# Attention with a banded mask and a routed MLP on one core: the output projection behind the first half's shift, its eviction between the exponentials, and three smaller moves

## The reference

```
x = x + attention(layernorm(x)) @ W_out + b_out      # 16 heads of 8, causal band of 32 keys
...
logits = layernorm(x) @ w_router                     # 8 choices, the best one is taken
sel    = expert e of 7 for a token, or none (choice 7)
x = x + 2 * prob(best) * expert_sel(h)               # (h @ w_up) * silu(h @ w_gate) @ w_down, 512 hidden
      + (h @ ws_up * silu(h @ ws_gate)) @ ws_down    # the shared expert, for all tokens
```

## Time and profile before

| what | value |
|---|---|
| runs | 309.22, 310.01 (median), 312.88 us |
| the profiled execution | 310.81 us, of which the span from first to last instruction is 308.8 us |
| mean granted TensorE clock | 0.991 |
| busy in the span | TensorE 293.2 us, VectorE 224.7, GpSimd 174.4, ScalarE 148.2 |
| attention, first maximum of round 0 to that of round 15 | 15.95 to 125.90 us |

### The profile page before, as it was taken

One profiled execution on the slowest core, in us unless ns is written; L12 is line 12 of the kernel. 1 busy time (PEld: TensorE's weight loads), 2 busy tenths in 40 slices (PEclk: granted clock), 3 DMA queues, 4 the chain that ended last, 5 costly groups with the idle time before them and its releaser, 6 DMA issues. The chain is left out here.

```text
span 308.8 us, 11890 instructions
## 1 busy us (share of the span) xinstructions
PE 293.2 (95%) x4834; PEld 242.9 (79%) x4834; DVE 224.7 (73%) x442; ACT 148.2 (48%) x230; POOL 174.4 (56%) x269
## 2 busy tenths in 40 slices
PE   8999999999799998889999999999989999999994
PEld 8846576657476666567888888889989999999993
DVE  5699999889779898876798655476677867865442
ACT  3544444545435476567273233244454554555530
POOL 6799476933214872391017777636467656655344
PEclk9999999999979999999999999999999999999998
DMA  7971414132313232109951233234244444334321
GB/s 195 338 194 55 109 44 119 47 108 53 97 42 109 50 98 62 56 15 392 345 158 55 91 114 111 88 73 86 62 85 95 87 88 96 73 80 82 72 51 27
DMA packets 52503, 32.46 MB, mean 105 GB/s; under 512 B 25424, under 2 KB 46676, under 8 KB 52450
## 3 DMA queue, kind: packets, MB, share of 16 engines
q1 hardware_dynamic: 47968, 23.18, 30.2%
q0 software_dynamic: 2880, 6.43, 6.0%
q10 hardware_dynamic: 1602, 2.10, 2.2%
HBM read 13.72 MB, written 11.95 MB: 83 GB/s over the span
## 5 line engine op out<-in xcount | busy, mean ns | idle before, releaser
L693 POOL DMA_INDIRECT out<-y,xn_base x38 | 38.6, 1015 | 38.9 <-DVE y L1390 37.7
L790 ACT ACTIVATE Pr<-psS 128x1024 f32<-128x1024 f32 x32 | 32.8, 1026 | 30.3 <-PE psS L1499 30.3
L1375 DVE TENSOR_TENSOR Pr<-psS,PT 128x512 f32<-128x512 f32 x38 | 26.1, 686 | 23.9 <-PE psS L1762 12.2
L907 ACT ACTIVATE PT<-psS 128x512 f32<-128x512 f32 x38 | 22.7, 597 | 38.9 <-PE psS L1762 30.2
L978 DVE TENSOR_REDUCE row_max<-psS 128x16 fp32r<-128x1024 f32 x32 | 37.7, 1218 | 4.8 <-PE psS L1487 4.7
L1760 PE MATMUL psS<-xT_hi,taken_parts 128*128 128x256 f32 x128 | 38.3, 299 | 0.0
L874 ACT ACTIVATE PT<-psS 128x512 f32<-128x512 f32 x32 | 19.1, 597 | 38.9 <-PE psS L1633 28.8
L1040 DVE STREAM_TRANSPOSE PT<-Pr 128x1024 f32<-128x1024 f32 x32 | 37.4, 1206 | 0.1
L1762 PE MATMUL psS<-xT_hi,taken_parts 128*128 128x256 f32 x128 | 36.1, 282 | 0.0
L536 POOL TENSOR_TENSOR rows<-rows,proj 128x256 f32<-128x256 f32 x15 | 10.9, 726 | 44.7 <-ACT proj L796 44.1
L1761 PE MATMUL psS<-xT_lo,taken_parts 128*128 128x256 f32 x128 | 35.9, 281 | 0.0
(11 more groups left out here) (227 smaller groups left out, 669.8 us busy)
## 6 DMA issues: line engine op xcount, KB each, us to landing
sorted_rows<-pad_rows SPq DMA_DIRECT2D x9, 528.0 KB, 6.1
xn_base<-sorted_rows SPq DMA_DIRECT2D x38, 66.0 KB, 1.9
rows<-in_L_attn_x SPq DMA_DIRECT2D x8, 256.0 KB, 6.0
xs<-sorted_rows SPq DMA_DIRECT2D x64, 32.0 KB
VD_even<-V SPq DMA_DIRECT2D x28, 72.0 KB, 2.8
VD_odd<-V SPq DMA_DIRECT2D x28, 72.0 KB, 2.5
w_sb<-in_L_ffn_w_gate ACTq DMA_DIRECT2D x1, 1792.0 KB, 12.8
Kx<-K SPq DMA_DIRECT2D x28, 64.0 KB, 2.2
```

Source lines behind the costliest of these rows:

```text
L693: pool.indirect_dma_start(out=out_list, out_offset=bass.IndirectOffsetOnAxis(tok_u[:, r, :], 0), in_=y[:, r, :], in_offset=None, bounds_ch ...
L790: nc.scalar.activation(Pr[:, half, :], psS[:, half, :], ACT.Exp, scale=SCALE).then_inc(exp_done, 1)
L1375: nc.vector.tensor_tensor(hs[:, k % PLACES, :], psS[:, k % 2, 0:512], sg[:, k % 2, :], ALU.mult).then_inc(eh_done, 1)
```

## The change

Four things are changed. In rounds 2 to 14 the output projection on TensorE stands behind the first half's shift (and behind `turn_x`) and no longer at the head of the round, and its copy on ScalarE stands behind the first exponential (and behind `evict_xnT`). The second block of idle matmuls has 24 in place of 48. The four copies that make `pick_h` go from GpSimd to VectorE, behind the statistics of the second batch, with a semaphore of their own. SP loads the fifth pair's tokens before it waits for the last scatters, where the four base loads stood ahead of them.

```diff
@@ SyncE
             for n in range(4):
                 load_pair(n)
+            load_pair(4)
             sp.wait_ge(base_scattered, 16 * LATE * TPB)
             for i in range(RING):
                 load_base(i, i, wait=False)
-            load_pair(4)
@@ GpSimd
             make(pool.memset(edge_h[:, :, BLK:], 0.0))
-            for g in range(NG):
-                w = slice(g * BLK, (g + 1) * BLK)
-                make(pool.tensor_copy(pick_h[w, :, :], ident[w, w].unsqueeze(1).to_broadcast([BLK, NJ, BLK])))
             make(pool.tensor_scalar(minus_ident[:, :], ident[:, :], -1.0, None, ALU.mult))
@@ ScalarE, pair(p)
-                if 2 <= p < NP - 1:
-                    evict_proj(p - 2)
                 exponentials(p, 0)
                 if p in (0, 2):
                     evict_xnT(n)
+                if 2 <= p < NP - 1:
+                    evict_proj(p - 2)
                 exponentials(p, 1)
@@ VectorE, after the statistics of the second batch
+            dve.wait_ge(filled, after["ident"])
+            for g in range(NG):
+                w = slice(g * BLK, (g + 1) * BLK)
+                nc.vector.tensor_copy(
+                    pick_h[w, :, :], ident[w, w].unsqueeze(1).to_broadcast([BLK, NJ, BLK])
+                ).then_inc(picks_ready, 1)
             dve.wait_ge(bias_mm, 1)
@@ TensorE
-            keep_warm(psS[:, 0, 0:P], 3 * WARM // 8)
+            keep_warm(psS[:, 0, 0:P], 3 * WARM // 16)
...
             pe.wait_ge(filled, after["masks"])
+            pe.wait_ge(picks_ready, NG)
...
-                if 2 <= p < NP - 1:
-                    project(p - 2)
                 if n == B:
                     turn_rows(2 * h + 1)
                 if p > 0:
                     weigh_values(p - 1, 0)
                 shift_scores(p, 0)
                 if p in (0, 2):
                     turn_x(n)
+                if 2 <= p < NP - 1:
+                    project(p - 2)
                 if p > 0:
                     weigh_values(p - 1, 1)
```

More of the change, by code:

```diff
@@ L237, in windowed_attention_top1_moe_kernel @@
         norm1_ready, first_normed = sem("norm1_ready"), sem("first_normed")
+        picks_ready = sem("picks_ready")
         first_k_ready, first_v_ready = sem("first_k_ready"), sem("first_v_ready")
```

## The result

The changed kernel takes 321.02 us in the median (320.06 to 323.36) against 310.33 us before (309.22 to 312.88), four runs of each: a ratio of 1.0384, 95% interval 1.0344 to 1.0423, so 10.7 us slower. The profiled execution has a span of 319.4 us and a mean granted clock of 0.993.

A forecast was written before the change was run, and what follows sets the result against it. VectorE was taken to set the quiet attention round, 6.33 us of work in 6.52. From the profiled 310.8 us, +16.8 (rounds) - 1.1 (start) - 1.2 (fifth pair) = 325.3, or 324.5 us as median; 8-in-10 range 319 to 332.

The forecast's parts named there:

- The mechanism: Rounds 2 to 14: copy behind first exponential makes VectorE's moments wait some 2 us for GpSimd's residual, near 26 us in all.
- Length of a round: Attention rounds 2 to 14: 6.33 us of VectorE work plus 2.03 us of later moments, 8.36 us a round.
- Round 2: Extra in round 2: input statistics (1.5 us for rounds 2 and 3 together) and the copy also behind `evict_xnT`, 0.5 us.
- The stop followed by half clock, +1.5: TensorE's longest stop, 2.0 us from 83.1, then 2.7 us at half clock: 1.5 us added, between 0 and 2.3.
- The start, -1.1: Kernel start: 24 idle matmuls fewer and picks on VectorE gain 1.1 us, between 0.4 and 1.4.
- my lower bound: Start gain of only 0.4 us, if the values' spreading DMAs land when they do today.
- The fifth pair, -1.2: SP's fifth-pair loads ahead of the scatter wait: VectorE's wait there goes, gain 1.2 us, between 0 and 1.3.
- The clock: Rival: VectorE-bound rounds idle TensorE, its clock falls to half; +6.5 us, 331 us, or 337 if scores become late; chance 0.12.
- the 0.5 us priced: Clock rival's estimate: at half clock a TensorE shift of 0.70 us takes some 0.5 us more in each of 13 rounds.
- TensorE's order: Rival: residual in time, but the projection's 0.64 us between the two shifts sets the price; +5.9, 313.5 us; chance 0.06.
- the covered wait: Rival: wait covered, rounds unchanged, only start and fifth pair change; 307.7 us; chance 0.04.
- TensorE's 0.64 us: Rounds 2 to 14: TensorE's 0.64 us is hidden by VectorE's wait; without that cover up to 0.6 us a round.

The follow-up runs named there:

- 12 tiny matmuls: Kernel before with start and fifth-pair edits, plus 12 tiny (32 x 32 by 32 columns) matmuls behind the 24 idle ones: 325.95 us, ratio 0.9890, on another chip.

## Why the prediction was right, and where it was off

The forecast was 324.5 us, 319 to 332; measured 321.0.

- *The mechanism*: right, to the wait. About 26 us of waiting for the residual was forecast, 26.2 us is in the trace; undoing the copy's place or moving the moments takes it away.
- *Length of a round*: forecast 8.36 us, measured 8.02 to 8.03. This is the largest mis-sized term, 13 x 0.34 = 4.4 us. Its error is one of reading. I chained reported durations: the exponential's 1.03 us to the copy (M+3.08), and VectorE's 6.33 us of work. On the chip each next instruction starts before the reported end of the one ahead: the copy 0.92 us behind the exponential's start, at M+2.90; the next maximum 2.25 us behind the start of two transposes of 2.33 us (78.07 to 80.32). The Trainium skill (Perfetto Trace Analysis, DVE / Act Engine Instruction) says that a reported end includes the acknowledgement of the write; the overlap of 0.08 to 0.11 us agrees.
- *Round 2*: 9.6 us by the terms of the forecast, 9.28 measured; the difference is the length of a round again, the extra statistics and the extra copy were sized right.
- *The stop followed by half clock, +1.5*: it did not happen in round 9 (8.02 us). Of the stops inside rounds 2 to 14 one of 0.64 us still shows, in a round of 8.08 us; the new slack covers the others. The two behind the start of round 15 are not covered, 0.89 and 1.60 us.
- *The start, -1.1*: the first maximum came 1.49 us sooner, round 2 0.95. As a part of the whole kernel's time it is worth nothing (ratio 1.0005). This step failed, though the total hides it: I carried a gain at the start to the end without asking what else the 24 removed instructions move. That is not all of it, since keeping the count didn't bring the gain back either. Part of the 1.49 us was never a gain: in the six profiles of kernels with the start as before, the first maximum lies anywhere from 14.98 to 16.16 us (mean 15.55) and round 2 begins at 30.24 in the mean; in the four with the changed start these are 14.63 and 29.81. By these means the edit is worth 0.9 us at the first maximum and 0.4 us at round 2. Where the rest goes stays open.

```profile
8.68 0.63 PE L1433 MATMUL psA<-ident,xn_base 128*128 128x128 f32 x4 [0.77 <-ACT xn_base L739]
...
9.57 1.45 DVE L1015 CAST pick_h<-ident 32x128 bf16<-32x128 f32 x4
...
14.46 1.23 DVE L976 TENSOR_REDUCE row_max<-psS 128x16 fp32r<-128x1024 f32 x1
...
23.12 0.76 PE L1523 MATMUL psO<-VD_even,PT 128*32 128x36 f32 x64 [1.16 <-DMA VD_even<-V]
```

  The rows are the changed kernel's first transpose of x, the four picks on VectorE (1.45 us for the four, as against 1.33 on GpSimd), the first maximum, and the first values, which now wait 1.16 us for their spreading DMAs, 0.46 before. That is the mechanism of my lower bound, and it takes part of the gain back.
- *The fifth pair, -1.2*: measured alone 1.7 us, 0.8 to 2.7. In the changed kernel the wait at the fifth pair is gone, and a later one of 1.09 us comes up at a later pair, within the bounds given:

```profile
236.69 0.43 DVE L1281 STREAM_TRANSPOSE xT<-xs 128x256 f32<-128x256 f32 x1
...
245.10 0.45 DVE L1281 STREAM_TRANSPOSE xT<-xs 128x256 f32<-128x256 f32 x1 [1.09 <-DMA xs<-sorted_rows]
```

- *The clock*: the rival did not decide, but it happened once. Where TensorE waited 1.26 and then 1.10 us in round 4, the granted clock fell to 0.50, the 1.2 GHz level, and rose again behind 52 us:

```profile
48.00:50.00 2.00, 1.12 (x3) 0.94 (x4) 1.96 (x2) 0.00 (x0) 0.00 (x0) 0.65 0.48 111
50.00:52.00 2.00, 2.00 (x69) 1.70 (x67) 0.00 (x0) 1.29 (x2) 0.49 (x1) 0.50 0.57 160
52.00:54.00 2.00, 2.00 (x13) 1.06 (x6) 1.67 (x7) 1.26 (x2) 2.00 (x6) 1.00 0.03 7
```

  A shift took 1.22 us there for 0.70, the 0.5 us priced, and round 4 took 8.59 us, 0.57 more than the rounds behind it. It was not the idle time of a usual round: round 4 alone had both gaps above 1 us. In rounds 5 to 14 they were at most 1.27 and 0.40 us, in round 3 0.90 and 1.10 us, and the clock stayed at 1.00.
- *TensorE's order and the covered wait*: both fell. With the copy moved alone the time is the same; with the projection moved alone the loss is that of the later copy. What the forecast said of TensorE's 0.64 us, hidden by the wait and up to 0.6 us a round without it, is borne out by the two kernels with late moments: 0.4 us in a quiet round.

In short, the rounds were priced 5.2 us too high (16.8 for 11.6), 4.4 of it for the length of a round and the rest for a stop that did not come, less the slow clock that came in round 4. On the other side, 1.2 us of gain was forecast behind the rounds and none is there in the profiled pair (182.9 us both): the stops of 0.89 and 1.60 us stand against the fifth pair's gain, which is argued from the rows and not isolated. So the total is nearer than its largest term by luck: one error took back part of the other. The forecast's own range, 321 to 328, holds the result at its edge.

## What to carry to other kernels

Before moving a step behind another, follow its result to the last engine that asks for it, and ask where in that engine's fixed order the question stands: here a copy moved by 2.3 us on an idle ScalarE made VectorE, the engine that sets the round, idle 1.8 us thirteen times. Chain starts, not durations, when you sum a round. And measure an edit's gain alone: a fifth pair loaded sooner was worth 1.7 us, and it vanished inside a change that cost seven times as much.

## What the runs showed of the hardware

TensorE stopped for up to 2.1 us at places that are fixed in its instruction stream, 256 recorded instructions apart: 24 matmuls fewer at the start moved them by exactly 24 matmuls in the program, 12 by 12. How long each stop lasts differed between kernels with equal places (0.19 to 1.02 us 21 matmuls before the end of one block). Each ended 1.24 to 1.55 us behind the end of a 16 KB packet on the profile's queue q8 instruction, so the length is how late that packet is. What sets its start is open: no run here varied it alone. Whether 12 tiny matmuls are better than 24 for a reason that would hold elsewhere is open too.
